# Cross attention's first scores: the mask of chunks 2 and 3 added by TensorE, one row-maximum instruction per chunk

## The reference, cut to what matters

```python
scores = jnp.einsum('bhqd,bhkd->bhqk', q, k) * scale
scores = jnp.where(mask[:, None, :, :] == 0, jnp.float32(NEG_INF), scores)
attn = jax.nn.softmax(scores, axis=-1)
```

## Time and profile before

| | |
|---|---|
| runs, median (lowest to highest) | 460.83 us (459.56 to 462.85) |
| span of the profiled execution | 457.5 us |
| TensorE matmuls, busy | 398.0 us, 87% of the span |
| TensorE weight loads, busy | 311.5 us, 68% |
| VectorE, busy | 385.7 us, 84% |
| ScalarE, busy | 359.9 us, 79% |
| GpSimd, busy | 329.2 us, 72% |
| masked maxima on VectorE (L895), custom instructions and accumulator reads | 112.8 and 42.3 us busy, 512 each |

### The profile page before, as it was taken

The page is one execution under the profiler, slowest core; times in us unless marked ns, Lnnn a source line. Parts: engine busy times, 40 slices in busy tenths (PEclk is TensorE's granted clock), DMA queues, the critical chain, the costliest instruction groups (busy, mean ns, idle before and its releaser), DMA issues. The chain is left out here.

```text
span 457.5 us, 18022 instructions
## 1 busy us (share of the span) xinstructions
PE 398.0 (87%) x5405; PEld 311.5 (68%) x5436; DVE 385.7 (84%) x1920; ACT 359.9 (79%) x962; POOL 329.2 (72%) x917
## 2 busy tenths in 40 slices
PE   3267879999999999999999999999999999877762
PEld 2245657777777777777877777778877777654430
DVE  4645467999999999999999999999999999888532
ACT  2214758899999999999999999999999998865542
POOL 6834667888888888888888888888888765654120
PEclk9998999999999999999999999999999999998655
DMA  6654577756666766676657675676567662422100
GB/s 190 162 146 100 140 188 184 173 149 172 173 159 160 191 163 168 150 195 172 170 148 196 175 175 153 164 181 170 152 158 189 165 164 80 101 78 77 30 6 13
DMA packets 100181, 67.27 MB, mean 147 GB/s; under 512 B 73269, under 2 KB 90421, under 8 KB 100085
## 3 DMA queue, kind: packets, MB, share of 16 engines
q1 hardware_dynamic: 98209, 64.08, 54.7%
q10 hardware_dynamic: 1876, 2.03, 1.5%
HBM read 46.08 MB, written 19.07 MB: 142 GB/s over the span
## 5 line engine op out<-in xcount | busy, mean ns | idle before, releaser
L895 DVE CUSTOM_DVE_ANT_0 biased<-bank,mask_bias 128x128 bf16<-128x128 f32 x512 | 112.8, 285 | 4.0 <-PE bank L1128 3.9
L900 DVE TENSOR_REDUCE neg_max_S<-bank 128x4 f32<-128x512 f32 x128 | 85.4, 675 | 21.1 <-PE bank L1128 20.4
L599 ACT ACTIVATE probs_S<-bank 128x512 f32<-128x512 f32 x128 | 72.7, 597 | 11.0 <-PE bank L1148 11.0
L599 ACT ACTIVATE probs_X<-bank 128x512 f32<-128x512 f32 x128 | 72.5, 590 | 7.0 <-PE bank L1148 6.4
L1128 PE MATMUL bank<-stack_k_S,stack_q_S 120*128 120x128 bf16 x512 | 50.5, 223 | 11.7 <-DMA stack_k_S<-scratch_S 11.0
L1148 PEld LDWEIGHTS bank<-stack_q_X,stack_k_X 74*128 74x128 bf16 x512 | 41.1, 100 | 16.6 <-issue 2.1
L1128 PEld LDWEIGHTS bank<-stack_k_S,stack_q_S 120*128 120x128 bf16 x512 | 38.6, 102 | 20.1 <-issue 11.9
L1148 PE MATMUL bank<-stack_q_X,stack_k_X 74*128 74x128 bf16 x512 | 51.4, 224 | 0.0
L1145 PE MATMUL bank<-ident_bf,mask_bias 128*128 128x512 bf16 x128 | 50.6, 396 | 0.0
L1128 PE MATMUL bank<-stack_k_X,stack_q_X 72*128 72x128 bf16 x512 | 45.3, 221 | 2.9 <-DMA stack_k_X<-scratch_X 1.7
L1166 PE MATMUL bank<-probs_X,v_aug_X 128*32 128x128 f32 x1024 | 42.4, 285 | 0.0
(11 more groups left out here) (165 smaller groups left out, 1178.6 us busy)
## 6 DMA issues: line engine op xcount, KB each, us to landing
stack_q_S<-scratch_S SPq DMA_DIRECT2D x32, 288.0 KB
stack_k_S<-scratch_S SPq DMA_DIRECT2D x32, 288.0 KB
stack_q_X<-scratch_X SPq DMA_DIRECT2D x32, 288.0 KB
stack_k_X<-scratch_X SPq DMA_DIRECT2D x32, 288.0 KB
scratch_S<-qk_parts_S SPq DMA_DIRECT2D x32, 192.0 KB, 2.7
scratch_X<-qk_parts_X SPq DMA_DIRECT2D x32, 192.0 KB, 2.7
scratch_S<-qk_parts_S SPq DMA_DIRECT2D x32, 64.0 KB, 1.7
ctxT<-ctx SPq DMA_DIRECT2D x8, 256.0 KB, 4.7
```

The source lines that it names most:

```text
L599: act.activation(probs[a][:, c, :], bank_b[c % 2][:, :], ACT.Exp).then_inc(sems["exp_" + a], 1)
L895: last = dve.tensor_tensor_reduce(biased[:, c, hh, :], quarter(bank_a[c % 2], hh), mask_bias[:, b % 2, :], -1.0, -2.0 * BIG, ALU.add, ALU.min,
L900: dve.tensor_reduce(neg_max[a][:, first_head(c):first_head(c) + 2 * HC - 1:2], bank_a[c % 2][:, :].rearrange("i (h j) -> i h j", h=HC), AX ...
```

## The change

One constant is changed. Chunks 2 and 3 of cross attention leave BIASED, so both branches that ask for it (in scores_a and in row_max) take their other side for these chunks.

```diff
-BIASED = (0, 1, 2, 3)
+BIASED = (0, 1)
```

## The result

The kernel with the change takes 471.42 us (median of four runs, 468.88 to 472.19); the kernel before, run beside it, 461.43 us (four runs, 459.56 to 462.85; three of them are those that were known). The ratio is 1.0207, with an interval of 1.0168 to 1.0246. The forecast was 473.9 us in a range of 466.5 to 477, slower.

What follows compares the result with a forecast made beforehand. The bound was taken as a VectorE–TensorE loop of 11.78 us a step. 11.9 + 0.6 + 0.9 - 0.3 = 13.1 on the 457.5 span gave 470.6, with 3.3 outside 473.9 us; range 466.5 to 477.

Steps and rivals of the forecast that it cites:

- The loop: VectorE from L930 to L1027, 7.71 us, then TensorE with one ScalarE copy back to L930, 4.07; together the 11.78 step.
- the late stage: Steps once self attention takes no new batch: L930 to L930 11.67 us, shorter by 0.11, taken as confirming the loop.
- 0.44 a step: Two added TensorE mask matmuls, 0.22 us each, between L1027 and L930, both counted in full; bounds 0 and 0.79.
- VectorE's two waits: VectorE waiting for TensorE each step: 0.3 to 0.5 us at chunk 3's reduction, 0.4 to 0.6 at L930.
- The 27 steps: Steps from L930 at 85.56 to L930 at 403.87, 318.31 us; 0.44 more in each, 11.9 us in all.
- The stray waits: 0.6 us in the 27 steps above 317.7; a longer step may swallow half, counted as -0.3.
- The steps ahead of them: Three steps with masked chunks but no feed forward, before the 27; 0.6 us added, bounds 0 to 1.3.
- The end: Two last steps without self attention, mask matmul spaced 0.42 at the lower clock; 0.9 us added, bounds 0 to 1.3.
- A: Rival, faster: VectorE is the bound, 64 chunks save 13 to 16 us, TensorE's 0.44 hides; about 446 us, chance 0.05.
- B: Rival, half: chunk 2's matmul hides because L1228 waits for o_norm_S, only chunk 3's 0.22 counts; 467.3 us, chance 0.10.
- C: Rival, no change: both matmuls hide, or the earlier VectorE gives the cost back elsewhere; 460.8 us, chance 0.04.
- D: Rival, more: something else becomes late too, or a matmul costs its row's 0.396; 482 us or above, chance 0.05.

Runs made afterwards that it cites:

- the runs on chunk 0: Kernel before with chunk 0's mask on TensorE, 460.71 us; with that mask left out, 460.84 us; with only TensorE's extra chunk 0 matmul, 464.12 us.
- VectorE's half alone: Kernel before with chunks 2 and 3 reduced once each on VectorE, their first-score mask left out, TensorE's work unchanged; 462.04 us, ratio 1.0033.

## Why the prediction was right, point by point

**The loop.** Right, and shown: a matmul added to L1027 to L930 lengthens the step by about what it takes of TensorE (both chunks, either chunk, with and without VectorE's part), and VectorE's saving in the same stretch is worth 0.00. Incomplete: from L930 to L1027 I named only VectorE's run. The path through down is equally long to about 0.04, and that through chunk 0's scores to about 0.14, as the runs on chunk 0 showed. It also spoils the late stage as a proof: there a shorter VectorE run made the step 0.11 shorter, from which I drew that VectorE's run alone holds that stretch. In the full steps, taking 0.2 from it brought 0.03.

**0.44 a step.** Measured 12.22 - 11.78 = 0.44, but out of three parts, of which one is 0.07 larger than I had it and another 0.06 to 0.07 smaller. That they cancel, and the sum came out to the hundredth, was luck. L1180 to L1228 grew by 0.22 as predicted. L1237 to L1245 grew by 0.29, since the mask matmul, spaced 0.21 itself, starts 0.13 behind the transpose of y, where chunk 3's scores started 0.05 behind it. L930 to L1027 shrank by 0.06 to 0.07, where I had it unchanged: in the kernel before, the two S reductions took 1.29 because the second waited a little for its scores; it started 0.68 behind the first, after the change 0.61 (medians), so the pair takes 1.22. My price of 0.65 for a reduction held that wait too. The likely reason is that L930 and so the reductions come later against TensorE; the runs show only that 7.64 or 7.65 stands wherever TensorE masks chunk 3, and 7.71 where it masks chunk 2 alone.

**VectorE's two waits.** Predicted 0.3 to 0.5 at chunk 3's reduction and 0.4 to 0.6 at L930; the rows show 0.44 and 0.47.

**The 27 steps.** The first and the last L930 of these steps in the trace after:

```profile
86.33 0.29 DVE L930 TENSOR_TENSOR x_all<-bank,x_all 128x128 f32<-128x128 f32 x1 [0.47 <-PE bank L1245]
...
416.91 0.29 DVE L930 TENSOR_TENSOR x_all<-bank,x_all 128x128 f32<-128x128 f32 x1 [0.47 <-PE bank L1245]
```

330.58 us, against 318.31: +12.27, where the sum had 11.9 - 0.3. The stray waits grew from 0.6 to 1.0 (330.58 less 24 x 12.22 + 3 x 12.11) rather than being swallowed. The steps ahead of them cost 86.33 - 85.56 = 0.77, predicted 0.6.

**The end.** Here the sum was off, and so was the step behind it. From the last L930 to the end of the span it was 457.5 - 403.87 = 53.6 before and 469.4 - 416.91 = 52.5 after: 1.1 less, where I had 0.9 more. I had counted the added matmuls at the lower clock and taken the clock itself as fixed. It was not. Three windows of the kernel before, from its last L930 on (columns as in the earlier trace rows):

```profile
404.00:416.00 12.00, 8.67 (x116) 5.71 (x116) 9.14 (x52) 8.53 (x20) 7.73 (x23) 1.00 0.27 74
416.00:428.00 12.00, 9.23 (x84) 6.09 (x85) 8.08 (x49) 5.60 (x12) 3.31 (x12) 0.72 0.18 52
428.00:440.00 12.00, 8.97 (x68) 5.21 (x69) 5.45 (x18) 6.16 (x12) 2.44 (x9) 0.60 0.12 34
```

And of the kernel after, likewise from its last L930 on:

```profile
417.00:429.00 12.00, 9.14 (x118) 5.91 (x118) 8.55 (x37) 8.17 (x19) 7.45 (x21) 1.00 0.28 75
429.00:441.00 12.00, 8.33 (x86) 5.64 (x87) 8.39 (x36) 5.97 (x13) 3.23 (x12) 0.86 0.18 51
441.00:453.00 12.00, 8.48 (x70) 4.94 (x71) 5.53 (x19) 5.87 (x11) 2.46 (x9) 0.72 0.12 33
```

In the second of these windows the granted clock is 0.72 before and 0.86 after, in the third 0.60 and 0.72. The tail so ran more of its work at the higher level, which fits its being shorter in spite of the added matmuls. But one profile of each kernel can't put this down to the change. The kernel without chunk 0's mask has TensorE's list of the kernel before, and its last L930 stands at 403.47; its first two windows are these:

```profile
404.00:416.00 12.00, 9.59 (x90) 6.90 (x84) 8.28 (x43) 6.79 (x17) 7.00 (x21) 0.73 0.27 74
416.00:428.00 12.00, 9.45 (x83) 6.45 (x83) 7.94 (x41) 5.70 (x11) 3.54 (x13) 0.64 0.17 53
```

The clock has fallen a window earlier there, and the tail lasts 459.2 - 403.47 = 55.7, 2.1 longer than in the kernel before, with no matmul added. So the end differs from one profile to another by more than the 0.9 that I had put in, and what the added matmuls cost there stays open.

**Outside the span.** I added 3.3 us, the median of the runs less the span of one profiled execution; these are different executions. After, span and time of one execution are 469.4 and 471.48, so 2.1 lie outside (about 2 in the other runs too); with that the sum would have been 472.7. Against the profiled 471.5 the forecast of 473.9 is 2.4 too high: the end -2.0, outside -1.2, the steps +0.7, the early ones +0.2, with rounding.

**The rivals.** A falls by the run with VectorE's half alone, B by chunk 2 alone, C by the result. D's second price, the row's 0.396 for a matmul, is not seen: each was spaced 0.21 or 0.22, and chunk 3's cost 0.29 with its later start.

## What to carry to other kernels

When several engines are full, look for the chain that leads from an instruction to itself a step later, and price a change by whether it stands on that chain, not by the busy time it saves: here 13.7 us less work on the busiest engine but one brought nothing, and 13.2 us more on TensorE cost 11.9. Then ask for each stretch of the chain how long the next longest path is; in a well balanced kernel it can be within a few hundredths, so that an addition costs in full while a saving brings nothing. For the time outside the span take span and time of the same execution.

## What the runs showed of the hardware that I had not expected

Behind the transpose of y the mask matmul started 0.13 us later when TensorE had stood idle ahead of the transpose (255.82 to 255.95; the same in the median of the steps), and 0.06 later when it had been busy up to it, as in the changed kernel with chunk 2's second scores moved (TensorE's timeline):

```profile
253.88 0.22 PE L1237 MATMUL bank<-ident_h,y_q 128*128 128x128 f16 x1
253.94 0.38 PE L1125 MATMUL bank<-mask_bias,ident_bf 128*128 128x512 bf16 x1
```

Chunk 3's scores started 0.05 behind the transpose although TensorE had been idle there too (261.43 to 261.48). The cause of the difference is open.

The granted clock at the end of the run falls at different points in profiles with the same list of TensorE: in the 12 us from 404 it was 1.00 in the kernel before, with TensorE busy 8.67 of 12 us, and 0.73 in the kernel without chunk 0's mask. The tails lasted 53.6 and 55.7 us.
